# Other PSUM banks for the down projections and a second table in four pieces, in a kernel of a quantised attention block beside a binary-difference FFN

## The reference, cut to what matters

```python
xn = layernorm(x)
# FFN branch: W = mean_w + coeff * sign(w - mean_w), coeff = mean|w - mean_w|, for w1, w2, w3
g = silu( (silu(xn @ W1.T) * (xn @ W3.T)) @ W2.T )
# attention-like branch: every W is a table of 16 values looked up by codes, times scales, plus B @ A (rank 16)
attn = (q(xn) + k(xn) + v(xn)) / 3
x1 = xn + o(attn)
s = x1 + down( silu(gate(x1)) * up(x1) )
out = x + s * g
```

## Time and profile before

| | |
|---|---|
| median of 3 runs | 547.72 us (547.15 to 548.33) |
| the profiled execution's own time | 545.55 us |
| its span in the profile | 543.8 us |
| TensorE busy | 520.8 us (96%) |
| VectorE busy | 441.2 us (81%) |
| ScalarE busy | 331.7 us (61%) |
| GpSimd busy | 100.7 us (19%) |
| granted TensorE clock | 1.00 |

### The profile page before, as it was taken

The page is one execution under the profiler, slowest core; times in us unless marked ns, Lnnn a source line. Parts: engine busy times, 40 slices in busy tenths (PEclk is TensorE's granted clock), DMA queues, the critical chain, the costliest instruction groups (busy, mean ns, idle before and its releaser), DMA issues.

```text
span 543.8 us, 6446 instructions
## 1 busy us (share of the span) xinstructions
PE 520.8 (96%) x2317; PEld 428.8 (79%) x2317; DVE 441.2 (81%) x511; ACT 331.7 (61%) x452; POOL 100.7 (19%) x109
## 2 busy tenths in 40 slices
PE   1899989999999999999999989999999999999997
PEld 1677778888888888888888767787888888888886
DVE  6999896978886998965898887998989889874446
ACT  2989868555745655446748655966886576455310
POOL 0311023102200220022003101500220031004590
PEclk9999999999999999999999999999999999999999
DMA  8999913224822391059209759871493368027503
GB/s 337 400 403 401 364 52 116 68 69 79 166 85 69 57 233 62 0 100 221 57 19 209 143 155 206 151 170 41 82 179 72 74 141 160 7 59 159 146 19 135
DMA packets 31759, 76.98 MB, mean 142 GB/s; under 512 B 3856, under 2 KB 7184, under 8 KB 31600
## 3 DMA queue, kind: packets, MB, share of 16 engines
q1 hardware_dynamic: 21648, 57.68, 33.7%
q0 software_dynamic: 9792, 18.88, 20.2%
q10 hardware_dynamic: 288, 0.02, 0.0%
HBM read 53.49 MB, written 2.10 MB: 102 GB/s over the span
## 4 chain that ended last, share of the span: by engine, by line
PE 70%; DVE 13%; ACT 7%; issue 5%; DMA 4%; SPq 0%; POOL 0%; DVEq 0%; ACTq 0%
PE up_ps L1539 19%; PE gate_pair L1539 18%; PE down_pair L1580 12%; PE down_ps L1580 6%; PE up_ps L1580 6%; DVE acc L1228 2%; PE side_ps L1605 2%; DMA codes<-in_codes 2%; DMA y<-y_part 2%; ACT ramp L807 1%; PE down_pair L1494 1%; PE up_ps L1678 1%; PE down_pair L1678 1%; PE gate_pair L1678 1%; DVE up_ps L1136 1%
## 5 line engine op out<-in xcount | busy, mean ns | idle before, releaser
L1539 PE MATMUL gate_pair<-xT,gu 128*128 128x512 f32 x696 | 165.2, 390 | 1.9 <-DVE gu L1107 1.5
L1539 PEld LDWEIGHTS gate_pair<-xT,gu 128*128 128x128 f32 x696 | 130.4, 188 | 29.7 <-DVE gu L1107 1.9
L1539 PE MATMUL up_ps<-xT,gu 128*128 128x512 f32 x624 | 147.3, 390 | 1.3 <-DVE gu L1093 0.7
L1539 PEld LDWEIGHTS up_ps<-xT,gu 128*128 128x128 f32 x624 | 116.7, 188 | 27.5 <-DVE h L1141 1.8
L613 POOL DMA_DIRECT2D y<-y_part x64 | 55.4, 896 | 323.7 <-ACT y_part L756 309.0
L743 ACT ACTIVATE h<-up_ps 128x512 fp32r<-128x512 f32 x52 | 31.1, 598 | 112.8 <-DVE up_ps L1136 60.4
L807 ACT ACTIVATE ramp<-codes,bend_bias 128x1536 f32<-128x1536 uint8 x56 | 88.1, 1579 | 3.5 <-DMA codes<-in_codes 3.5
L1580 PE MATMUL down_pair<-h,dn 128*128 128x512 f32 x327 | 80.6, 389 | 0.5 <-DVE h L1141 0.5
L1228 DVE SCALAR_TENSOR_TENSOR acc<-ramp,acc 128x1536 f32<-128x1536 f32 x42 | 73.7, 1754 | 5.1 <-ACT ramp L807 4.5
L1580 PEld LDWEIGHTS down_pair<-h,dn 128*128 128x128 f32 x327 | 61.3, 188 | 13.7 <-DVE dn L1093 0.9
L1141 DVE TENSOR_TENSOR h<-up_ps,h 128x512 fp32r<-128x512 f32 x52 | 35.8, 688 | 20.6 <-ACT h L743 20.6
(11 more groups left out here) (204 smaller groups left out, 600.6 us busy)
## 6 DMA issues: line engine op xcount, KB each, us to landing
y<-y_part POOLq DMA_DIRECT2D x64, 256.0 KB, 5.1
scale<-in_scales SPq DMA_DIRECT2D x28, 384.0 KB, 5.5
scan_w<-in_w SPq DMA_DIRECT2D x15, 512.0 KB, 11.4
base<-in_mean SPq DMA_DIRECT2D x10, 768.0 KB, 4.8
...
```

The source lines that it names most:

```text
L1539: last = nc.tensor.matmul(ps[:, :], w[:, w_part, hc * P:(hc + 1) * P], xT[:, x_part, hc, th * HALF:(th + 1) * HALF], start=(hc == 0 and w_ ...
```

## The change

Five edits.

1. **Scan.** The up products of chunk 2 go to `down_pair` instead of `up_ps`, those of chunk 3 to `up_ps` instead of the gate banks. The waits follow: chunk 2 waits for the silu of chunk 0, chunk 3 for the low parts of chunk 0. `total(DOWN)` moves from behind the ups of chunk 2 into the first up of chunk 3, behind its sixth matmul.
2. **D0.** Its tiles use `down_ps2`, the gate banks and `down_pair` in turn. The first three tiles are made in two rounds: chunks 0 and 1 for all three, then chunk 2. VectorE and ScalarE make units 8 and 9 and their low parts first; `h_low(1, 1)`, unit 10 and `h_high(2, 0)` are placed around that.
3. **Order of banks** in the other down stages: `down_ps0, down_ps2, up_ps0, down_ps1, up_ps1` (D4, behind X: `down_ps0, down_ps1, down_ps2, up_ps0, up_ps1`, with X's own banks reordered to match). `rank_gu` waits for the last tile that used `down_pair`, not for all eight; the ups wait for the last tile that used their bank.
4. **Tables.** ScalarE makes the high part with the scale in the same instruction (one instead of two), VectorE's low rows scale too. The second half is made in four pieces of 512, 512, 512 and 256 columns: ScalarE at the ends of phases 15 to 18, VectorE in phases 16 to 19.
5. **Loads.** The second half of the table is loaded in two transfers behind the codes of chunk 16, with no wait for X. The 2 MB copy of x1 into `y2` stands behind the codes of chunk 17 instead of those of chunk 18, and no longer waits for the table.

```diff
-DOWN_AFTER_X1 = {0: 2, 2: 5, 3: 7, 4: 8}
+DOWN_AFTER_X1 = {0: 1, 1: 2, 2: 5, 3: 7, 4: 8}
+DOWN0, DOWN1, DOWN2, UP0, UP1, GATE0, GATE1 = range(7)
+DOWN_RING = [(DOWN2, GATE0, GATE1, DOWN0, DOWN1) if g == 0 else (DOWN0, DOWN1, DOWN2, UP0, UP1) if g == FFN_GROUPS - 1
+             else (DOWN0, DOWN2, UP0, DOWN1, UP1) for g in range(len(GROUPS))]
+LATE_PHASES = [B0 + 1, B0 + 2, B0 + 3, B0 + 4]
+def bank_free(g, bank):
+    return TT * g + max(t for t in range(TT) if DOWN_RING[g][t % RING] == bank) + 1
...
         def up_bank(k, th):
-            return gate_ps[th] if k in (1, 3) else up_ps[th]
+            return gate_ps[th] if k == 1 else down_ps[th] if k == 2 else up_ps[th]
-        x1_ps = [down_ps[2], down_ps[0], gate_ps[0], gate_ps[1], down_ps[1], side_ps, up_ps[0], up_ps[1]]
+        x1_ps = [down_ps[0], down_ps[1], gate_ps[0], gate_ps[1], down_ps[2], side_ps, up_ps[0], up_ps[1]]
...
-            sp.wait_ge(x1_done, TT)
-            sp.dma_start(B_gu_late[0:ROWS3, 0:INTER], B_gu_in[:, 1, :]).then_inc(B_gu_loaded, 16)
+            sp.wait_ge(ffn_made, 3 * (B0 - FIRST))
+            sp.dma_start(B_gu_late[0:ROWS3, :, :].rearrange("p a n -> p (a n)"), B_gu_in[:, 1, 0:6 * 2 * P]
+                         ).then_inc(B_gu_late_loaded, 16)
+            sp.dma_start(B_gu_end[0:ROWS3, :], B_gu_in[:, 1, 6 * 2 * P:INTER]).then_inc(B_gu_late_loaded, 16)
-                if k == B0 + 3:
-                    sp.wait_ge(B_gu_lo, 2)
+                if k == B0 + 2:
                     sp.wait_ge(x1_lo, TT)
                     sp.wait_ge(y_out, TT * FFN_GROUPS)
                     sp.dma_start(y2[:, :, :], xT[:, HI, :, :].bitcast(f32)).then_inc(y2_copied, 16)
...
+            def late_high(n):
+                act.wait_ge(B_gu_late_loaded, 32)
+                nc.scalar.activation(late_split(n, 0, ROWS3), late_raw(n, 0, ROWS3), ACT.Copy, scale=1.0 / UNIT_STEP
+                                     ).then_inc(B_gu_hi, 1)
...
                 h_make(k, 0)
+                if k - 1 in LATE_PHASES:
+                    late_low_rows(LATE_PHASES.index(k - 1))
...
             unit_make(8)
-            h_low(1, 1)
             unit_make(9)
-            unit_make(10)
-            h_make(2, 0)
             unit_low(8)
             unit_low(9)
+            h_low(1, 1)
+            h_make(2, 0)
+            unit_make(10)
+            h_low(2, 0)
             unit_low(10)
-            h_low(2, 0)
...
                     if k == FIRST:
-                        pe.wait_ge(h_lo, half_count(k - 1, th))
+                        pe.wait_ge(y_out, bank_free(0, GATE0 + th))
...
+                elif k == 2:
+                    pe.wait_ge(silu_done, half_count(0, th))
                 else:
-                    pe.wait_ge(h_lo, half_count(k - 2 if k < FIRST else k - 1, th))
+                    pe.wait_ge(h_lo, half_count(0 if k < FIRST else k - 1, th))
...
-                elif t >= 3:
-                    pe.wait_ge(h_lo, half_count(NEWEST[g], t - 3))
+                elif DOWN_RING[g][t] in (UP0, UP1):
+                    pe.wait_ge(h_lo, half_count(NEWEST[g], DOWN_RING[g][t] - UP0))
...
+            def first_down():
+                for ks in (GROUPS[0][:2], GROUPS[0][2:]):
+                    for t in range(FIRST_TILES):
+                        if ks[0] == 0 and t == 2:
+                            pe.wait_ge(h_lo, half_count(1, 1))
+                        for k in ks:
+                            if t == 0:
+                                pe.wait_ge(dn_lo, k + 1)
+                                pe.wait_ge(h_lo, half_count(k, 0))
+                            for w_part, h_p in PASSES:
+                                last = nc.tensor.matmul(down_bank(0, t)[:, :], dn[:, k, w_part, t * P:(t + 1) * P],
+                                                        h_part(k, h_p, 0), start=(k == 0 and w_part == h_p == HI),
+                                                        stop=(k == GROUPS[0][-1] and w_part == LO))
...
-                    pe.wait_ge(y_out, TT * DOWNS_BEFORE[k])
-                pe.wait_ge(B_gu_lo, half + 1)
+                    pe.wait_ge(y_out, max(bank_free(DOWNS_BEFORE[k] - 1, DOWN0), bank_free(DOWNS_BEFORE[k] - 1, DOWN1)))
+                pe.wait_ge(B_gu_lo, 1 + half * len(LATE_PIECES))
...
-                project(c, UP, 0)
+                project(c, UP, 0, DOWN if c == FIRST - 1 else None, 1)
                 project(c, UP, 1)
-                if c == 2:
-                    total(DOWN)
```

More of the change, by code:

```diff
@@ L36 @@
 RING = 5
+FIRST_TILES = 3
+LATE_PIECES = [(0, 512), (512, 1024), (1024, 1536), (1536, 1792)]
 ROWS3 = 96
@@ L147, in block_kernel @@
         scale_qkv = sb("scale_qkv", [P, 4, 3, 8])
-        with nc.sbuf_tensor("acc2", [P, TRIO], f32) as acc2:
+        with nc.sbuf_tensor("acc2", [P, TRIO], f32) as acc2, \
+                nc.sbuf_tensor("B_gu_late", [P, 6, 2 * P], f32) as B_gu_late:
             pass
@@ L207, in block_kernel @@
         with nc.sbuf_tensor("y2", [P, HC, TOKENS], f32) as y2:
-            pass
-        with nc.sbuf_tensor("B_gu_late", [P, 2 * TOKENS], f32) as B_gu_late:
             pass
@@ L414, in last_bank @@
         def last_bank(half):
-            return (down_bank(TT - 1) if half == 0 else side_ps)[:, half * HALF // 2:(half + 1) * HALF // 2]
+            return (down_bank(LAST, TT - 1) if half == 0 else side_ps)[:, half * HALF // 2:(half + 1) * HALF // 2]
         def tile_slice(t):
@@ L755, in y_evict @@
                         act.wait_ge(y_added[q % Y_SLOTS], 16 * (q // Y_SLOTS))
-                nc.scalar.activation(place, down_bank(t)[:, :], ACT.Copy, scale=1.0 if g < FFN_GROUPS else UNIT_STEP
+                nc.scalar.activation(place, down_bank(g, t)[:, :], ACT.Copy, scale=1.0 if g < FFN_GROUPS else UNIT_STEP
                                      ).then_inc(y_out, 1)
@@ L1001, in _ @@
                         A_down_high()
-                    if stage == B0:
-                        B_gu_scale(1)
-                        B_gu_high(1)
+                    if stage in LATE_PHASES:
+                        late_high(LATE_PHASES.index(stage))
                     if stage == 17:
@@ L1453, in _ @@
                         A_down_low()
-                    if stage == B0:
-                        B_gu_low_rows(1)
                 else:
@@ L1542, in project @@
                                                 stop=(hc == HC - 1 and w_part == LO))
-                    if hc == 2 and total_within is not None:
+                    if hc == total_at and total_within is not None:
                         total(total_within)
@@ L1579, in down @@
                     for w_part, h_p in PASSES:
-                        last = nc.tensor.matmul(down_bank(t)[:, :], dn[:, k % DN_SLOTS, w_part, hq * P:(hq + 1) * P],
+                        last = nc.tensor.matmul(down_bank(g, t)[:, :], dn[:, k % DN_SLOTS, w_part, hq * P:(hq + 1) * P],
                                                 h_part(k, h_p, th), start=(k == ks[0] and w_part == h_p == HI),
@@ L1659, in down_stage @@
             def down_stage(g):
-                for t in range(TT):
+                if g == 0:
+                    first_down()
+                for t in range(FIRST_TILES if g == 0 else 0, TT):
                     down(g, t)
```

67 lines of the change are left out of this document (38 added, 29 removed).

## The result

The changed kernel takes 542.88 us (median of 7 runs, 540.42 to 543.09), the kernel before, run beside it on the same chip, 547.15 (7 runs, 545.14 to 548.33): ratio 0.9924, 95% interval 0.9899 to 0.9948, 4.3 us faster. The forecast was 542.0 in a range of 540.2 to 544.2. The runs of both kernels lie in two groups some 2.4 us apart, and the cause sits in the first 35 us (experiments 1 and 2). The profiled execution before (545.55 us) is of the lower group, the one after (542.70) of the upper, so the two must not be set against each other as a whole.

The account below looks back on a forecast made before the run. TensorE was taken as the bound, so only its idle time could be won. 1.65 + 0.6 + 2.75 + 1.05 - 0.3 = 5.75 us, off the 547.72 median, gave 542.0; range for 8 in 10: 540.2 to 544.2.

Parts of the forecast that it names:

- What bounds the kernel, and the sum's start: Whole kernel: TensorE busy 520.8 of 543.8 us, only its idle time can be won; gain taken off a 547.72 median.
- Scan and D0: Scan's end: D0 starts at 73.36, chunk 4's gate near 90.2 behind ScalarE's eviction; gain 1.65 us.
- First rank product behind D4: Behind D4: the rank product waits for tile 6's eviction instead of tile 7's; gain 0.6 us of 1.05 lost.
- Phases 15 and 16: Ups and gates before D5: `gu_low` of chunk 16 no longer late once table work leaves; gain 2.75 us.
- Rank product behind D5: Behind D5: the rank product no longer waits for a late eviction; gain 1.05 us, bounds 0.8 and 1.05.
- now tile 5 decides: Behind D5: the rank product waits only for tile 5, evicted by 347.48, before TensorE is ready at 349.01.
- The pieces: Phases 17 to 19: VectorE's table pieces delay `h_low`; 0.3 us charged, bounds 0.6 gained and 1.2 lost.
- the two mechanisms: Stall for `h_low` at chunk 19's ups stays, growing a little; D6's tile 2 may wait for `h_low(19, 0)`.
- The last two terms: Rank product behind D5, gain 1.05 us, and table pieces in phases 17 to 19, loss 0.3, added separately.
- The late codes: ScalarE waited 3.46 us for codes sharing transfers with a burst of adds; some 0.5 us of VectorE lead expected.
- Moved transfers: Table load and 2 MB copy placed among scales and codes of chunks 16 to 18; nothing charged.
- The first rival: VectorE is the true limit from 300 to 380 us; gain about 3.3, 544.4 us; chance 0.13.

Follow-up runs that it names:

- experiments 1 and 2: The kernel before and the changed kernel, each with 22 idle small matmuls ahead of the first products; 544.98 and 540.59 us.
- warmed kernels: Kernels with 22 idle small matmuls added at the start; here the kernel before at 544.98 us and the changed kernel at 540.59 us.
- w_rounds: Changed kernel with the idle start matmuls, D0's first three tiles made in one round instead of two; 542.65 us.
- w_total: Changed kernel with the idle start matmuls, the one-column matmul for DOWN back between the ups of chunks 2 and 3; 541.34 us.
- w_gate: Changed kernel with the idle start matmuls, D0's first three banks in the order gate 0, gate 1, down 2; 539.92 us.
- w_onepiece: Changed kernel with the idle start matmuls, the table's whole second half made in phase 14 again, in parts of 1,536 and 256 columns; 541.39 us.
- w_ring: Changed kernel with the idle start matmuls, the old order of banks back in D1 to D3 and D5 to D8; 540.28 us.
- w_before: Kernel before the change with 22 idle small matmuls ahead of the first products; 544.98 us.
- w_after: Changed kernel with 22 idle small matmuls ahead of the first products; 540.59 us.
- w_newring: Kernel before with the idle start matmuls, plus only the new bank order of D5 to D8 and the rank product's shorter wait; 544.67 us.
- w_d6: Changed kernel with the idle start matmuls, D0's banks gate 0, gate 1, down 2, and VectorE's last three table pieces at D6's end; 538.29 us.
- w_copy: Changed kernel with the idle start matmuls, the 2 MB copy of x1 behind the codes of chunk 18 again; 540.66 us.

## Why the forecast was right in its time, and which step of it failed

- **The time.** 542.88 against a forecast of 542.0, but 0.6 of that nearness is luck: the gain was forecast as 5.75 and measured as 4.27, and the median of the kernel before came out at 547.15 instead of the 547.72 from which the forecast took it off. It is luck too that both medians fell into the upper group (four runs of seven before, five of seven after); a median of the lower one would have been near 540.5, close to the lower edge of the range.
- **What bounds the kernel, and the sum's start.** Held. The median moved by 4.3 us for a gain of 4.4 between the warmed kernels.
- **Scan and D0: 1.65.** Right to 0.01 at the gate of chunk 4 (92.03 to 90.38), and by its own chain: D0 at 73.47 (forecast 73.4), the gate at 90.38 behind an eviction (forecast 90.2). 1.51 arrive at phase 14. `w_rounds` and `w_total` show the parts, `w_gate` that ScalarE held 0.66 us back.
- **First rank product behind D4: 0.6.** 0.48, and it keeps 0.2 us of wait (2.93 us behind its gate, where 2.72 are work).
- **Phases 15 and 16: 2.75.** Exactly 2.75 (1.99 to 4.74 in the table), and `w_onepiece` brings 1.40 of it back.
- **Rank product behind D5: 1.05.** The size is right at the place (0.96), the cause isn't. I wrote "now tile 5 decides". In the changed kernel tile 7 would not have been late either (`w_ring`): the eviction was late in the kernel before because ScalarE followed a VectorE that was behind, and the table's leaving phase 14 had cured that already. ScalarE's first eviction of D5 starts 3.92 us after D5 in `w_before`, 2.47 in `w_after`, and 3.92 again in `w_onepiece`, where the table is back in phase 14 and the eighth eviction ends at 346.41, 0.9 us after the rank product could start. In the kernel before the new order does make the rank product earlier, and D6 is not earlier for it (`w_newring`).
- **The pieces: -0.3.** This is the step that failed. From the rank product behind D5 to the end of D6, the stall at the ups of chunk 19 and the new one at D6's tile 2 take 1.52 us more than in `w_before`, beyond my bound of 1.2, and `w_d6` wins them all back by moving 1.6 us of VectorE's work. Against the profiled execution from which I made the term it is 0.95 (49.16 to 50.11 us), within the bound, because that one had a stall of 0.6 at chunk 19 that `w_before` does not have. I had the two mechanisms and their places, but thought that VectorE's lead of 1.2 us at D5 and the end of the late codes would pay for the pieces, and took two of them for 1.36 us where they cost 1.7. The `h_low` ahead of D6 starts 4.56 us earlier in `w_after` than in `w_before` (373.12 and 377.68), and D6 starts 4.58 us earlier, though TensorE had been 5.70 ahead: VectorE sets that start. So as long as the pieces stand there, the 0.96 won at the rank product is waited away again. The last two terms had to be one: 0.75 by my sum, -0.56 measured.
- **The late codes.** I counted 0.5 us for them. ScalarE's wait fell from 2.86 us in `w_before` to 0.74 in `w_after`, but with 2.86 us of it `w_before` lost nothing at the ups of chunk 19 (375.85 to 381.30, 5.45 us for 24 matmuls). By these two traces the 0.6 us there in the profiled execution belonged to that execution, with its 3.46 us: its `h_low` of the earlier trace rows starts 0.77 us later than that of `w_before`. No kernel tried it by itself.
- **Moved transfers: 0.** Held, by `w_copy`, for the copy; the table's load was not tried by itself.
- **The first rival** (VectorE the limit from 300 to 380 us, gain 3.3) was half right: it let the 2.75 us be lost too, which they were not, but had the place of the loss. The measured 4.3 lies between it and the forecast.
